# Weight-part stores on SyncE's queue, and a later, denser schedule for the bursts that prepare a slice

## The chip, the cores and the metric

The kernel runs on one core of one Trainium2 chip. The metric is the device time of the program in microseconds (us), smaller is better. Five things matter here: TensorE (PE) multiplies, VectorE (DVE) and ScalarE (ACT) move and cast, GpSimd (POOL) subtracts, and SyncE (SP) only waits and issues DMAs. Each engine takes its instructions strictly in order; they meet at semaphores.

## The reference

```
masked_w = weight * mask[None, :, :]                 # weight (8, 512, 512), mask (512, 512)
w_bot    = einsum('bg,got->bot', y, masked_w)        # y (128, 8): one mixed weight matrix for each of 128 samples
out      = x + (einsum('bnt,bot->bno', x, w_bot) + bias)   # x (128, 128, 512)
```

For each sample b, eight weight matrices are mixed by y[b], and x[b] (128 rows of 512) is multiplied by the mixture; x itself is added (the kernel adds the identity to the weights instead), and a bias. Everything is float32.

## The kernel before

**Tiling.** The 512 outputs are cut into 4 slices of 128, the 128 samples into 4 blocks of 32. A *unit* is a slice of a block; there are 16 units. A unit is 8 *groups* of 4 samples, so there are 128 *steps* n = 0..127, and step n of unit u = n // 8 runs group n. A group is 16 fp32 products, which the profile shows as 32 matmul records (L526), that multiply x (tile `xs`) by the mixed weights in `wbot`. Below, T(n) is the moment at which TensorE begins step n.

**Bursts.** `wbot` of the next unit is made while the current unit runs. That is 8 *bursts* a unit, 4 chunks each (L509, 8 small bf16 matmuls a chunk, 32 a burst), from weight parts in a `ring` of 6 slots against `ydiag`. Burst b belongs to unit b // 8. Within a step TensorE runs the bursts of that step first and then the group. `BEFORE` and `bursts_before(n)` say which bursts stand at step n: one at each step (burst n + 8), except in unit 0, where bursts 8 to 15 stand at steps 3 to 7. The 512-column results lie in 6 PSUM buffers (`S1B`), and are copied to `wbot` by ACT (chunks 0, 1, 3; L348) and DVE (chunk 2; L425). `wbot` is written in place: a chunk (c, k) of the next unit may be written only when sample 4c + k of the current unit has been multiplied (`chunk_ready`). The first group of a unit waits for the last burst's chunks (`evicted`). A third copy, DVE's `duplicate` (L420), fills 32 of the 98 rows of a ring slot from 32 others, and TensorE waits for it.

**Weight parts.** fp32 weights are split into three bf16 parts once, in 32 *tiles* of raw weights, and kept in DRAM (`w_parts`); a unit of a later block reads them again. Four tiles are a *half*, that is the weights of 4 bursts. Units 1, 2, 3, 4 need tiles 0 to 7, 8 to 15, 16 to 23, 24 to 31. A tile goes through: load (`load_raw`, SP), multiply by the mask (`multiply_mask`, DVE, L409), first cast (`cast_w1`, ACT, L330), subtraction (`subtract_w1`, L186), second cast (`cast_w2`, ACT, L334) and second subtraction (`make_w3`, L190), store (`store_parts`, ACT, L342). The subtractions are DVE's for tiles 0 to 7 (`EARLY`) and POOL's afterwards. `TILES_AT` says at which step a tile is cast: tile t at step t - 9 (8 and 9 at step 0), so tile 31 at step 22. Tiles 0 to 7 are done in a prologue, next to the first slice's weights, which are made from `xs` by another path (L488, L490).

**Order of the queues.** SP runs a list written out by hand: first-slice weights, raw tiles, x groups 0 and 1, the first ring loads, and then a loop over n. In its iteration n it loads raw tiles of step n + 2, x groups, and ring slots whose previous burst stands at or before step n. `load_burst` waits until the four tiles of its half are stored (`stored`, L181) and until the slot's previous burst is through TensorE. A raw load (L229) waits until tile t - 8 is done with. ACT runs, per step: second cast of the last step's tile, evictions of chunks 0 and 1, first cast, store of output n - 1 (L353), store of parts, evictions of 2 and 3. DVE runs, per step: `duplicate` of bursts up to `AHEAD` = 2 steps on, mask of the tile, evictions of chunk 2, bias (L436). TensorE's group n waits for x and for the bias of n - 2.

Of the kernel before, what the change touches and what calls it, by code (L numbers as in the profile page):

```python
# [4 lines left out]
P = 128  # L5
# [4 lines left out]
W = 32  # L10
# [10 lines left out]
CO = 16  # L21
CS = SL // CO
OJ = 2
# [21 lines left out]
TILES_AT = {0: (8, 9), **{n: (n + 9,) for n in range(1, 23)}}  # L45
# [4 lines left out]
AHEAD = 2  # L50
BEFORE = {0: (), 1: (), 2: (), 3: (8,), 4: (9,), 5: (10, 11), 6: (12, 13), 7: (14, 15)}
X_AHEAD = 4
# [3 lines left out]
def bursts_before(n):  # L56

    return BEFORE.get(n, (n + GROUPS,) if n + GROUPS < BURSTS else ())
# [13 lines left out]
for _n in range(STEPS):  # L72
    LAST_BURST.append(max((LAST_BURST[-1], *bursts_before(_n))))

# [18 lines left out]
def cond_resid_kernel(nc: bass.Bass, x, w, mask, y, bias, pick, eye, w0, mask0, sel, ident, out, scratch):  # L93
# [6 lines left out]
    with ctx:  # L100
# [16 lines left out]
        sel_sb = sb("sel_sb", [P, CO], fp32)  # L117
        y0_sb = sb("y0_sb", [P, W], fp32)
        ident_sb = sb("ident_sb", [P, P], bf16)
# [14 lines left out]
        s_ident = sem("s_ident")  # L134
# [82 lines left out]
        def _(eng):  # L217
# [19 lines left out]

            def load_burst(b):
# [86 lines left out]
        def _(eng):  # L325
# [10 lines left out]
            def store_parts(t):  # L336
                h, i = divmod(t, PER_HALF)
                eng.wait_ge(s_p2, t + 1)
                p3_made(eng, t)
                at = scratch[h, i * TG, 0, 0, :]  # L340
                to = bass.AP(tensor=at.tensor, offset=at.offset, ap=[[TW, P], [OJ * HCOLS, TG * 3], [1, TW]])
                eng.dma_start(to, parts[:, t % PARTN, :, :, :].rearrange("p g j c -> p (g j) c"))\  # L342
                   .then_inc(s_store[t % PARTN], 16)

# [5 lines left out]
            def store_out(n):  # L350
# [4 lines left out]
            eng.dma_start(y0_sb[:, :], bass.AP(tensor=y.tensor, offset=y.offset,  # L355
                                               ap=[[0, CO], [YC, NG], [1, W]])).then_inc(s_first, 16)
            eng.dma_start(sel_sb[:, :], sel).then_inc(s_first, 16)
            eng.dma_start(ident_sb[:, :].bitcast(fp32), ident).then_inc(s_ident, 16)
# [9 lines left out]
            for c in range(CS):  # L368
                evict(c, 0)
                cast_w1(c)  # L370
                evict(c, 1)
                evict(c, 2)
                cast_w2(c)
                evict(c, 3)
                store_parts(c)
            before = ()
            for n in range(STEPS):
# [12 lines left out]
                for t in before:  # L390
                    store_parts(t)
# [7 lines left out]
            for t in range(TILES - PARTN, TILES):  # L399
                stored(eng, t)  # L400

        @block.vector
        def _(eng):
# [37 lines left out]
            eng.wait_ge(s_first, 16 * 2)  # L441
            eng.tensor_tensor(yblk.rearrange("p (b o) -> p b o", o=CO), y0_sb[:, :].unsqueeze(2).to_broadcast([P, W, CO]),  # L442
# [165 lines left out]
```

## Time and profile before

| | us |
|---|---|
| median of 3 runs | 691.91 |
| lowest, highest | 691.61, 697.16 |
| the profiled execution's own time | 693.39 |
| its span | 691.6 |
| TensorE busy / share | 630.8 / 91% |
| VectorE busy | 371.2 |
| ScalarE busy | 268.8 |
| GpSimd busy | 78.3 |
| mean DMA rate | 231 GB/s |

The span goes from the first to the last instruction; 1.8 us of the execution's time lie around it. Busy times of different engines overlap. "x4096 | 499.1, 281 | 16.6 <-DMA xs<-in_x 13.3" means 4096 instructions, 499.1 us busy in all, 281 ns each (they are pipelined, so the sum is less than count times length), and 16.6 us in which the engine stood idle in front of them, most of it until that DMA.

### The profile page before, as it was taken

The page shows a single profiled execution, that of the slowest core. Times are in us where ns is not written, and L with a number is a line of the kernel's source. Part 1 is how long each engine was busy: PE and PEld are TensorE (multiplying, and loading weights), DVE is VectorE, ACT ScalarE, POOL GpSimd, SP SyncE. Part 2 cuts the span into 40 slices and gives each one's busy share as a digit, 9 for nine tenths or more (in the row PEclk, how much of TensorE's full clock was granted, in tenths as well). Part 3 has the DMA queues.
Part 4 walks back from the last instruction along what each step waited for, and adds up shares of the span by engine and source line. Part 5 has one row for each costly group of instructions (what it writes and reads, how often), then busy time and mean ns, then how long its engine had stood idle before and what let it go on. Part 6 is the DMA issues. An engine that isn't in the chain of part 4 may idle for free.

```text
span 691.6 us, 18831 instructions
## 1 busy us (share of the span) xinstructions
PE 630.8 (91%) x8008; PEld 606.5 (88%) x8008; DVE 371.2 (54%) x433; ACT 268.8 (39%) x449; POOL 78.3 (11%) x63
## 2 busy tenths in 40 slices
PE   5973559989879997999999999999999999999998
PEld 2453559889879987999999999999999999999997
DVE  4734546656765534665565555655565546555421
ACT  3631146445444432343434433343434343434300
POOL 2204422545540000000000000000000000000000
PEclk9996779988989999999999999999999999999999
DMA  9988976777876985655557985555559966553122
GB/s 233 354 252 247 359 253 237 260 233 252 268 239 223 334 294 234 241 208 194 172 184 261 331 290 240 235 189 176 175 191 335 311 243 244 209 191 136 63 77 77
DMA packets 67167, 159.80 MB, mean 231 GB/s; under 512 B 6714, under 2 KB 32412, under 8 KB 55068
## 3 DMA queue, kind: packets, MB, share of 16 engines
q1 hardware_dynamic: 22752, 112.08, 47.3%
q10 hardware_dynamic: 44332, 46.52, 20.0%
q8 instruction: 64, 1.05, 0.6%
q14 instruction: 19, 0.16, 0.1%
HBM read 112.44 MB, written 46.14 MB: 229 GB/s over the span
## 4 chain that ended last, share of the span: by engine, by line
PE 67%; DMA 19%; DVE 4%; SPq 3%; issue 3%; ACTq 2%; ACT 2%; POOL 0%; DVEq 0%
PE ps L526 53%; PE ps L509 13%; DMA ring<-w_parts 8%; DMA raw<-in_w 6%; DMA w_parts<-parts 4%; DMA xs<-in_mask 1%; ACTq L342 1%; DVE raw L409 1%; SPq L255 1%; SPq L256 1%; ACTq L353 1%; ACT wbot L348 1%; DVE wbot L425 1%; DVE raw L186 1%; ACT parts L330 0%
## 5 line engine op out<-in xcount | busy, mean ns | idle before, releaser
L526 PE MATMUL ps<-wbot,xs 128*128 128x128 f32 x4096 | 499.1, 281 | 16.6 <-DMA xs<-in_x 13.3
L526 PEld LDWEIGHTS ps<-wbot,xs 128*128 128x128 f32 x4096 | 478.9, 196 | 18.3 <-DMA xs<-in_x 13.5
L348 ACT ACTIVATE wbot<-ps 128x512 f32<-128x512 f32 x384 | 232.6, 611 | 313.3 <-PE ps L526 269.2
L420 DVE COPY ring<-ring 32x4096 bf16<-32x4096 bf16 x120 | 156.3, 1304 | 62.4 <-DMA ring<-w_parts 59.6
L509 PE MATMUL ps<-ydiag,ring 98*128 98x64 bf16 x3840 | 137.2, 194 | 32.4 <-ACT wbot L348 21.8
L425 DVE COPY wbot<-ps 128x512 f32<-128x512 f32 x128 | 88.2, 690 | 142.7 <-PE ps L526 141.8
L509 PEld LDWEIGHTS ps<-ydiag,ring 98*128 98x128 bf16 x3840 | 131.0, 99 | 37.6 <-ACT wbot L348 24.5
L436 DVE TENSOR_TENSOR staged<-ps,bias_sb 128x512 f32<-128x512 f32 x128 | 88.1, 689 | 41.0 <-PE ps L526 30.0
L409 DVE TENSOR_TENSOR raw<-raw,mask_sb 128x512 f32<-128x512 f32 x32 | 27.3, 856 | 56.5 <-DMA raw<-in_w 56.2
L186 POOL TENSOR_TENSOR raw<-raw,parts 128x512 f32<-128x512 f32 x24 | 29.2, 1218 | 115.7 <-ACT parts L330 115.7
L330 ACT ACTIVATE parts<-raw 128x512 bf16<-128x512 f32 x32 | 20.0, 627 | 55.4 <-DVE raw L409 55.2
L190 POOL TENSOR_TENSOR parts<-raw 128x512 bf16<-128x512 f32 x24 | 40.6, 1692 | 1.9
L488 PE MATMUL ps<-staged,xs 128*128 128x512 f32 x64 | 31.0, 623 | 8.3 <-DMA ident_sb<-in_ident 7.4
L488 PEld LDWEIGHTS ps<-staged,xs 128*128 128x128 f32 x64 | 12.6, 201 | 23.4 <-issue 13.9
L334 ACT ACTIVATE parts<-raw 128x512 bf16<-128x512 bf16 x32 | 20.1, 628 | 15.7 <-POOL raw L186 11.4
L186 DVE TENSOR_TENSOR raw<-raw,parts 128x512 f32<-128x512 f32 x8 | 5.5, 686 | 5.3 <-ACT parts L330 5.3
L414 DVE TENSOR_TENSOR xs<-xs 128x512 f32<-128x512 f32 x8 | 5.6, 698 | 3.6 <-DMA xs<-in_mask 3.6
L190 DVE TENSOR_TENSOR parts<-raw 128x512 bf16<-128x512 f32 x8 | 5.5, 691 | 0.3
L348 ACT ACT_TABLE_LOAD x1 | 1.3, 1283 | 6.7 <-issue 6.7
L442 DVE TENSOR_TENSOR staged<-y_sb,sel_sb 128x512 f32<-128x512 f32 x1 | 0.7, 693 | 5.9 <-DMA sel_sb<-in_sel 5.9
L490 PE MATMUL ps<-ident_sb 128*128 128x512 bf16 x8 | 3.3, 411 | 0.0
L490 PEld LDWEIGHTS ps<-ident_sb 128*128 128x128 bf16 x8 | 0.8, 104 | 2.2 <-issue 2.2
(11 smaller groups left out, 8.8 us busy)
## 6 DMA issues: line engine op xcount, KB each, us to landing
ring<-w_parts SPq DMA_DIRECT2D x240, 256.0 KB
xs<-in_x SPq DMA_DIRECT2D x32, 1024.0 KB, 17.7
out<-staged ACTq DMA_DIRECT2D x128, 256.0 KB, 6.8
w_parts<-parts ACTq DMA_DIRECT2D x32, 384.0 KB, 9.3
raw<-in_w SPq DMA_DIRECT2D x32, 256.0 KB, 10.3
xs<-in_w SPq DMA_DIRECT2D x8, 256.0 KB, 8.2
xs<-in_mask SPq DMA_DIRECT2D x8, 256.0 KB, 9.6
ring<-in_eye SPq DMA_DIRECT2D x120, 16.0 KB
```

The source lines that it names most:

```text
L186: eng.tensor_tensor(at, at, parts[:, t % PARTN, :, 1, :], ALU.subtract).then_inc(done, 1)
L190: eng.tensor_tensor(parts[:, t % PARTN, :, 0, :], raw[:, t % RAWN, :, :], high_half(t), ALU.subtract).then_inc(done, 1)
L330: eng.activation(parts[:, t % PARTN, :, 1, :], raw[:, t % RAWN, :, :], ACT.Copy).then_inc(s_p1, 1)
L334: eng.activation(parts[:, t % PARTN, :, 2, :], high_half(t), ACT.Copy).then_inc(s_p2, 1)
L348: eng.activation(chunk_place(b, k), chunk_sums(b, k), ACT.Copy).then_inc(s_ev_a, 1)
L409: eng.tensor_tensor(at, at, mask_sb[:, h % 2, :].unsqueeze(1).to_broadcast([P, TG, TW]), ALU.mult).then_inc(s_mul, 1)
L420: eng.tensor_copy(ring[QUAD:2 * QUAD, i, :], ring[0:QUAD, i, :]).then_inc(s_dup, 1)
L425: eng.tensor_copy(chunk_place(b, k), chunk_sums(b, k)).then_inc(s_ev_v, 1)
L436: eng.tensor_tensor(staged[:, n % OUTB, :].rearrange("p (b o) -> p b o", b=GB), ps2[n % S2B][:, :].rearrange("p (b o) -> p b o", b=GB), bi ...
L488: ins = eng.matmul(to, xs[:, RAW0 + c, k, :], yblk, start=True, stop=(k > 0))
L509: ins = eng.matmul(ps1[at % S1B][:, g * W * OJ:(g + 1) * W * OJ], ring[:, i, k * CW + g * P:k * CW + (g + 1) * P], ydiag[:, first:first + ...
L526: ins = eng.matmul(ps2[n % S2B][:, b * SL:(b + 1) * SL], xs[:, load % GROUPS * GB + b, k, :], at, start=(k == 0), stop=(k == KT - 1))
```

## The change

- `store_parts` moves from ACT to SP. In the prologue the eight stores stand between the loads: 0 and 1 before x 0, 2 and 3 before x 1, 4 before the first ring load, 5, 6 and 7 between x 2 and x 4. All eight first x groups are now issued in the prologue; the first raw tile after tile 7 (tile 8) comes after all of them and after six ring loads.
- In SP's loop, iteration n first loads raw tiles of step n + 3 (`RAW_AHEAD`), then x, then ring slots, and last stores the tile of step n - 1. A ring load is issued only once the iteration before has issued the stores of its half (`tiles_of`, `kept`).
- `TILES_AT`: tile t is cast at step t - 4, so tiles 8 to 31 stand at steps 4 to 27.
- `LATE`: in units 0 to 3, the bursts of the next unit stand at the unit's steps 2, 3, 4, 5, 6, 6, 7, 7 (none at its steps 0 and 1). From unit 4 on it is one a step, as before.
- `AHEAD` is 1. In the prologue, second casts and second subtractions come one tile later.
- Three small first loads (part of y, `sel`, the identity) become one (`first`). ACT no longer waits for the last stores at the end.

```
-TILES_AT = {0: (8, 9), **{n: (n + 9,) for n in range(1, 23)}}
+TILES_AT = {t - 4: (t,) for t in range(EARLY, TILES)}
-AHEAD = 2
-BEFORE = {0: (), 1: (), 2: (), 3: (8,), 4: (9,), 5: (10, 11), 6: (12, 13), 7: (14, 15)}
-X_AHEAD = 4
+AHEAD = 1
+RAW_AHEAD = 3
+LATE = {0: (0, 0, 1, 1, 1, 1, 2, 2), ... 3: (0, 0, 1, 1, 1, 1, 2, 2)}
 def bursts_before(n):
-    return BEFORE.get(n, (n + GROUPS,) if n + GROUPS < BURSTS else ())
+    u, gg = divmod(n, GROUPS)
+    if u in LATE:
+        first = (u + 1) * CS + sum(LATE[u][:gg])
+        return tuple(range(first, first + LATE[u][gg]))
+    return (n + GROUPS,) if n + GROUPS < BURSTS else ()
+def tiles_of(b):
+    u, c = divmod(b, CS)
+    return (half_of(u % SLICES, c) + 1) * PER_HALF if u <= SLICES else 0
 @block.sync
+            def store_parts(t):                      # was ACT's
+                h, i = divmod(t, PER_HALF)
+                eng.wait_ge(s_p2, t + 1)
+                p3_made(eng, t)
+                ...
+                eng.dma_start(to, parts[:, t % PARTN, :, :, :]...).then_inc(s_store[t % PARTN], 16)
...
+            load_raw(7)
+            store_parts(0)
+            store_parts(1)
             load_x(0)
-            load_raw(7)
+            store_parts(2)
+            store_parts(3)
             load_x(1)
-            for b in range(CS, CS + 4):
-                load_burst(b)
-            load_raw(8)
-            load_raw(9)
+            store_parts(4)
+            load_burst(CS)
             load_x(2)
-            load_raw(10)
+            store_parts(5)
+            load_burst(CS + 1)
             load_x(3)
+            store_parts(6)
+            store_parts(7)
+            load_burst(CS + 2)
+            load_x(4)
+            load_burst(CS + 3)
+            load_x(5)
             load_burst(CS + 4)
+            load_x(6)
             load_burst(CS + 5)
+            load_x(7)
             loaded = CS + RING
+            kept = EARLY
             for n in range(STEPS):
-                for t in TILES_AT.get(n + 2, ()):
+                for t in TILES_AT.get(n + RAW_AHEAD, ()):
                     load_raw(t)
-                if n + X_AHEAD < GROUPS:
-                    load_x(n + X_AHEAD)
                 ...
-                while loaded < BURSTS and loaded - RING <= LAST_BURST[n + 1]:
+                while loaded < BURSTS and loaded - RING <= LAST_BURST[n + 1] and tiles_of(loaded) <= kept:
                     load_burst(loaded)
                     loaded += 1
+                for t in TILES_AT.get(n - 1, ()):
+                    store_parts(t)
+                    kept = t + 1
 @block.scalar
...
-                cast_w2(c)
+                if c:
+                    cast_w2(c - 1)
                 ...
-                store_parts(c)
...
-                for t in before:
-                    store_parts(t)
 @block.vector
...
-                subtract_w1(eng, c, s_rest_v)
-                make_w3(eng, c, s_p3_v)
                 if c + 1 < CS:
                     multiply_mask(c + 1)
+                if c:
+                    make_w3(eng, c - 1, s_p3_v)
+                subtract_w1(eng, c, s_rest_v)
```

## Rows read from the trace of the kernel before

**Rows 1.** The page: TensorE's granted clock in tenths, in 40 slices.
```profile
PEclk9996779988989999999999999999999999999999
```
**Rows 2.** The page: the costliest group, line, engine, count, busy, mean ns, idle before.
```profile
L526 PE MATMUL ps<-wbot,xs 128*128 128x128 f32 x4096 | 499.1, 281 | 16.6 <-DMA xs<-in_x 13.3
```
**Rows 3.** TensorE's timeline in an undisturbed stretch: start us, length us, instruction.
```profile
286.85 1.10 PE L509 MATMUL ps<-ydiag,ring 98*128 98x64 bf16 x32
...
291.44 1.10 PE L509 MATMUL ps<-ydiag,ring 98*128 98x64 bf16 x32
292.37 0.80 PE L526 MATMUL ps<-wbot,xs 128*128 128x128 f32 x5
```
**Rows 4.** TensorE's timeline in unit 0 and at the start of step 8.
```profile
62.56 5.38 PE L526 MATMUL ps<-wbot,xs 128*128 128x128 f32 x32 [13.29 <-DMA xs<-in_x]
...
81.23 1.09 PE L509 MATMUL ps<-ydiag,ring 98*128 98x64 bf16 x16 [8.23 <-ACT wbot L348]
82.13 5.80 PE L526 MATMUL ps<-wbot,xs 128*128 128x128 f32 x32
...
116.06 1.10 PE L509 MATMUL ps<-ydiag,ring 98*128 98x64 bf16 x32
```
**Rows 5.** TensorE's timeline at steps 14, 23 and 32.
```profile
156.69 6.06 PE L526 MATMUL ps<-wbot,xs 128*128 128x128 f32 x32
...
201.09 0.39 PE L509 MATMUL ps<-ydiag,ring 98*128 98x64 bf16 x8 [2.92 <-DVE wbot L425]
...
247.02 1.10 PE L509 MATMUL ps<-ydiag,ring 98*128 98x64 bf16 x32
```
**Rows 6.** VectorE's timeline: a mask that waited for its raw tile.
```profile
151.96 0.69 DVE L409 TENSOR_TENSOR raw<-raw,mask_sb 128x512 f32<-128x512 f32 x1 [7.06 <-DMA raw<-in_w]
```
**Rows 7.** SyncE's waits: line, releaser, us in total, times, longest.
```profile
SPq L181 <- DMA w_parts<-parts: 109.0, 9, 15.8
```
**Rows 8.** Windows: stretch, length, busy of five engines, granted clock, DMA share, GB/s.
```profile
0.00:80.00 80.00, 49.88 (x248) 31.13 (x248) 37.40 (x52) 27.89 (x48) 19.33 (x22) 0.89 0.94 280
34.00:80.00 46.00, 23.27 (x188) 19.39 (x186) 17.11 (x21) 10.87 (x19) 10.78 (x7) 0.81 0.90 270
...
247.00:692.00 445.00, 433.84 (x5890) 431.52 (x5888) 232.79 (x273) 162.20 (x265) 0.00 (x0) 1.00 0.59 210
```
**Rows 9.** The page's DMA queues: SyncE's, packets, MB, share of 16 engines' span.
```profile
q1 hardware_dynamic: 22752, 112.08, 47.3%
```
**Rows 10.** The steps of a tile on ScalarE around the end of step 7.
```profile
115.03 0.62 ACT L330 ACTIVATE parts<-raw 128x512 bf16<-128x512 f32 x1
```
**Rows 11.** The same tile's subtractions on GpSimd, and one slowed beside VectorE.
```profile
115.72 1.16 POOL L186 TENSOR_TENSOR raw<-raw,parts 128x512 f32<-128x512 f32 x1 [4.41 <-ACT parts L330]
116.97 1.04 POOL L190 TENSOR_TENSOR parts<-raw 128x512 bf16<-128x512 f32 x1
...
121.79 1.90 POOL L190 TENSOR_TENSOR parts<-raw 128x512 bf16<-128x512 f32 x1
```
**Rows 12.** Landing times of one store of parts, issued at 120.30 us (tile view).
```profile
DMA to landing us min/median/max: 3.1/3.1/3.1
```
**Rows 13.** Landing time of the store issued at 124.73 us.
```profile
DMA to landing us min/median/max: 15.5/15.5/15.5
```
**Rows 14.** The ring load of burst 16 on SyncE and the duplicate that waited for it.
```profile
101.67 0.67 SPq L255 DMA_DIRECT2D ring<-w_parts  x1
...
106.35 1.22 DVE L420 COPY ring<-ring 32x4096 bf16<-32x4096 bf16 x1 [0.57 <-DMA ring<-w_parts]
```
**Rows 15.** The second loading of x: landing of the load issued at 243.39 us, and TensorE behind it.
```profile
DMA to landing us min/median/max: 29.3/29.3/29.3
...
264.69 1.09 PE L509 MATMUL ps<-ydiag,ring 98*128 98x64 bf16 x32 [1.84 <-DVE wbot L425]
```
**Rows 16.** The page: TensorE's first products, busy, mean ns, idle before.
```profile
L488 PE MATMUL ps<-staged,xs 128*128 128x512 f32 x64 | 31.0, 623 | 8.3 <-DMA ident_sb<-in_ident 7.4
```
**Rows 17.** ScalarE's queue: a DMA issue that took long.
```profile
82.58 6.53 ACTq L353 DMA_DIRECT2D out<-staged  x1
```

More of the change, by code:

```diff
@@ L90, with cond_resid_kernel @@
         A_DONE.append(A_DONE[-1] + (not on_vector(_b, _k)))
-def cond_resid_kernel(nc: bass.Bass, x, w, mask, y, bias, pick, eye, w0, mask0, sel, ident, out, scratch):
+def cond_resid_kernel(nc: bass.Bass, x, w, mask, y, bias, pick, eye, w0, mask0, first, out, scratch):
     fp32 = mybir.dt.float32
@@ L116, in cond_resid_kernel @@
         ydiag = sb("ydiag", [KALL, NB, OJ], bf16)
-        sel_sb = sb("sel_sb", [P, CO], fp32)
-        y0_sb = sb("y0_sb", [P, W], fp32)
-        ident_sb = sb("ident_sb", [P, P], bf16)
+        first_sb = sb("first_sb", [P, W + CO + P // 2], fp32)
+        y0_sb = first_sb[:, 0:W]
+        sel_sb = first_sb[:, W:W + CO]
+        ident_sb = first_sb[:, W + CO:].bitcast(bf16)
         bias_sb = sb("bias_sb", [P, NO], fp32)
@@ L236, in load_first @@
                    .then_inc(s_w0[c], 16)
+            def store_parts(t):
+                h, i = divmod(t, PER_HALF)
+                eng.wait_ge(s_p2, t + 1)
+                p3_made(eng, t)
+                at = scratch[h, i * TG, 0, 0, :]
+                to = bass.AP(tensor=at.tensor, offset=at.offset, ap=[[TW, P], [OJ * HCOLS, TG * 3], [1, TW]])
+                eng.dma_start(to, parts[:, t % PARTN, :, :, :].rearrange("p g j c -> p (g j) c"))\
+                   .then_inc(s_store[t % PARTN], 16)
             def load_burst(b):
@@ L353, in store_out @@
                 eng.dma_start(out[u, :, gg, :], staged[:, n % OUTB, :]).then_inc(s_out[n % OUTB], 16)
[L355 to L358, printed above, removed]
+            eng.dma_start(first_sb[:, :], first).then_inc(s_first, 16)
             for q in range(3):
@@ L398, in _ @@
                 eng.wait_ge(s_out[i], 16 * (STEPS // OUTB))
-            for t in range(TILES - PARTN, TILES):
-                stored(eng, t)
         @block.vector
@@ L439, in add_bias @@
                                   ALU.add).then_inc(s_o, 1)
[L441 to L443 removed]
+            eng.wait_ge(s_first, 16)
+            eng.tensor_tensor(yblk.rearrange("p (b o) -> p b o", o=CO), y0_sb.unsqueeze(2).to_broadcast([P, W, CO]),
+                              sel_sb.unsqueeze(1).to_broadcast([P, W, CO]), ALU.mult).then_inc(s_yblk, 1)
             multiply_first(0)
@@ L482, in first_burst @@
                     eng.wait_ge(s_yblk, 1)
-                    eng.wait_ge(s_ident, 16)
+                    eng.wait_ge(s_first, 16)
                 eng.wait_ge(s_mul0, c + 1)
@@ L567 @@
     }
-    a["sel"] = np.repeat(np.eye(CO, dtype=np.float32), NG, axis=0)
-    a["ident"] = np.where(np.eye(P), 0x3F80, 0).astype(np.uint16).view(np.float32)
+    ident = np.where(np.eye(P), 0x3F80, 0).astype(np.uint16).view(np.float32)
+    a["first"] = np.concatenate([np.tile(y[:, :W], (CO, 1)), np.repeat(np.eye(CO, dtype=np.float32), NG, axis=0), ident],
+                                axis=1)
     pick = np.zeros((KALL, 3 + OJ), np.float32)
@@ L598 @@
     cond_resid_kernel(nc, aps["x"], aps["w"], aps["mask"], aps["y"], aps["bias"], aps["pick"], aps["eye"],
-                      aps["w0"], aps["mask0"], aps["sel"], aps["ident"], out, scratch)
+                      aps["w0"], aps["mask0"], aps["first"], out, scratch)
     r = run_bass_kernel_spmd(nc, [arrays], core_ids=[0])
```

15 lines of the change are left out of this document (4 added, 11 removed).

## The prediction

> **What bounds the kernel now.** I read the page's slices first: after the first third TensorE's clock stands at 9 or more everywhere, before it it falls to 6 again and again [rows 1]. The costliest group is the fp32 product, and nearly all its waiting is one wait for x [rows 2]. So I asked TensorE's timeline what a step costs when nothing disturbs it: bursts begin at 286.85 and 291.44 and the group behind the latter at 292.37, so a step is 4.59 us, of which the burst is 0.94 and the group 3.65 [rows 3]. From step 32 on the kernel is that and little else: 433.8 of 445 us busy [rows 8]. All that a schedule can win lies ahead of it, in two stretches.
>
> Opening, up to T(8) = 116.1. TensorE stood 13.3 us for x 2, 8.2 us for an eviction behind a blocked ScalarE queue, and more of that kind [rows 4]. After such a wait a group takes 5.80 instead of 3.82 us as the timeline counts it, about 2.0 more: these are the two levels, 1.2 and 2.4 GHz, of the granted clock, which is 0.89 of full on average up to 80 us and 0.81 from 34 to 80, while the DMA engines are 0.94 busy up to 80 us, at 280 GB/s [rows 4, 8].
>
> Steps 8 to 31, from 116.1 to T(32) = 247.0: 130.9 us [rows 4, 5], where 24 steps of 4.59 are 110.2. The 20.7 us more are visible as VectorE waiting for a raw tile that SyncE loaded late (7.06 us at 151.96), with evictions and bias behind it in its queue [rows 6]; TensorE then waits for the eviction, 2.92 us at step 23 [rows 5]. SyncE was late because it stood 109 us in nine waits until a half was stored [rows 7].
>
> **The change, part by part.**
>
> *Opening.* x 2 no longer stands behind four ring loads and three raw tiles, so its 13.3 us go. What is late next is tile 8. It is cast at step 4, and its load now stands behind all eight x groups and six ring loads. What must have moved by then: first weights and their masks 4.2 MB, raw tiles 0 to 8 with masks 2.6, x 8.4, ring 3.1, stores of eight tiles 3.1, outputs of five steps 1.3: 22.7 MB (1 KB = 1024 B; sizes are the tiles' own). In the old kernel 80 us moved 280 GB/s, 22.4 MB [rows 8], so it lands at L = 80; I take 79, since there is slightly less of slow small stuff on the queues. TensorE has nothing to wait for before step 6 (step 0 at about 40 as before, then two groups alone and four steps of 4.59, and some loss between the slices: about 67) and then stands: VectorE's step 4 waits for tile 8, and behind it in its queue are the eviction of burst 10, the bias of step 4 (for group 6) and the duplicates of bursts 12 and 13. From L on VectorE needs 0.69 for the mask, 0.69 eviction, 0.69 bias, 1.22 each for two duplicates, 0.69 mask of tile 9; ScalarE casts it (0.62), waits for GpSimd's 1.16 and casts again (0.62) before it evicts burst 12, which burst 13 needs. That is 9.1 us from L to the start of group 6. Then 5.8 for the cold group, and 5.5 for step 7 with its two bursts: T(8) = L + 20.5 = 99.5. **Term: -16.5.** Bounds: at 344 GB/s (112.08 MB in 47.3% of 691.6 us, SyncE's queue [rows 9]) from about 35 us, L is 69 and the term -26.5; with 270 GB/s, the rate between 34 and 80 us [rows 8], and 4 us of idle DMA while SyncE waits for stores 3 and 7, L is 87 and the term -8.5.
>
> *The round trip of a half, six times.* This is the heart of it. The first half of units 2, 3 and 4 ends with a tile cast at the last step of a unit and is needed by a burst at the next unit's step 2; the second half ends at step 3 and is needed at step 6. In the old schedule there were six steps between, now three. Take tile 11, step 7, burst 16 at step 10. ScalarE's first cast stands behind the eviction of the second burst's chunk 1, which must wait for sample 29; in the old trace the cast of that step stands at 115.03, 1.03 us before T(8) [rows 4, 10]. GpSimd's subtractions are 1.16 and 1.04 or 1.90 us; the second of step 7's tile ended at 118.0, 1.95 after T(8) [rows 11]. I say T(8) + 2.4 for the store. A store with nothing behind it landed in 3.1 us [rows 12]; with loads issued behind and around it, in 15.5 [rows 13]. Here SyncE stands still behind the store, so 3.3. Then 0.4 for waking and the small identity load, 4.65 from the issue of the ring load until its duplicate could start [rows 14], 1.22 for the duplicate: T(8) + 12.1. Steps 8 and 9 now have no bursts and last 3.65 each, so TensorE is there at T(8) + 7.3. It waits 4.8 (the last evictions of the old unit, which no burst covers any more at steps 8, 16 and 24, lie inside that), and then runs a group at the low clock, 2.0.
>
> Second half, tile 15, step 11, bursts 20 and 21 at step 14: VectorE's step 11 starts 0.8 after T(11), duplicate 1.22, mask 0.69, cast 0.62, subtractions 1.16 and 1.90: store at T(11) + 6.3; 3.3 + 0.4 + 4.65 + 1.22 make 16.0, against 13.8 for three steps: 2.2. But VectorE was held in step 13, with the mask of tile 17 behind the duplicates, and TensorE needs for burst 21 what ScalarE evicts of burst 20 only after the second cast of tile 17: after the mask about 4.7 us go by until the group starts (in the old trace mask at 151.96, group at 156.69 [rows 5, 6]). So group 14 starts 6.5 us after burst 20 instead of 1.9: 4.6 more, and again 2.0 for the clock. A unit pays 4.8 + 2.0 + 2.2 + 4.6 + 2.0 = 15.6, three units **46.8**.
>
> Bounds of this term: with the store landing at 3.1 and a ring load at 3.5 (my estimate: little more than such a store), it is still 30; with 6.4 and 6 us for the two it is 75. Nothing excludes the lower end, and no gain is in it.
>
> *The second x loads in unit 3.* They are issued at steps 25 to 32. In the old kernel no tile was under way then; now half four is stored and read back at steps 24 to 30, on the same queue, behind up to three x groups of 1 MB. Loads of x landed there after up to 29.3 us [rows 15]. I put 3 us on the first half and 8 on the second: **11**, between 3 and 20.
>
> *What goes.* The 20.7 us of steps 8 to 31 go in full: raw tiles are now loaded before SyncE stands for the stores, three steps ahead, and a load that finds the queue empty has three steps. So steps 8 to 31 take 110.2 + 46.8 + 11 = 168.0 instead of 130.9: **+37.1**.
>
> *After step 32.* The old kernel loses 11.2 us there [rows 8], most of it in waits of 1 to 2 us behind the x loads, where VectorE stood for a ring slot it needed only two steps on [rows 15]. `AHEAD` of 1 makes it stand one step later. **-6**, between 0 and -9.
>
> *Edits taken together at nothing.* One first load for three: TensorE waited 7.4 us for the identity [rows 16], and its first product needs the masked first weights, ready at about the same time; within 0.3. The store waits at the end of ScalarE's queue were long over. Moving 32 issues off ScalarE frees its queue: but the outputs stay there, and one of them held the queue 6.53 us [rows 17]; what held TensorE in the opening is counted above. The Trainium skill, page DMA: Bandwidth & Descriptors, section Issuing engines are not separate DMA queues, says that issuing from several engines saves only the time of issue. By that rule alone the move would change no landing time and would be worth the few long issues; the rows say otherwise, 3.1 against 15.5 us for a store of the same size [rows 12, 13], so I let a store's landing depend on what is queued with it.
>
> **Sum:** -16.5 + 37.1 - 6 = +14.6. Against the profiled execution, 693.4, that is 708.0; it was 1.5 above the median, so on the median's scale 706.5. I say **706**.
>
> **Rivals.**
>
> *A, the round trip is hidden (faster).* Place: from the first cast of a half's last tile to the duplicate of its first burst. It decides whether these take less than 9.2 us (first half) or 13.8 from the step's start. For it: the 4.65 us of the ring load is a single reading, and an empty queue could be quicker. Against: cast, subtractions and one store landing alone are 6 us, which leaves 3 for a ring load and its duplicate [rows 10 to 12]. Then the 46.8 fall away: 706 - 47 = 659. Chance 0.10.
>
> *B, DMA is quicker than I allow.* L is 69, x is absorbed in unit 3 (3 instead of 11), ring loads land in 3.5: -10 - 8 - 7: 681. For it: x-heavy stretches of the page move over 340 GB/s. Chance 0.18.
>
> *C, stores behind loads.* SyncE's list puts a store behind whatever was issued before it: the six critical stores land in 6.4 or more, ring loads in 6, x in unit 3 costs 20: by the upper bounds above 706 + 28 + 9; not all six will meet them, say 728. For it: the 15.5 of [rows 13] and 29.3 of [rows 15]. The Trainium skill, same page, section Queues, rings and completion order, says that each ring is consumed in order and an engine takes turns between queue rows: a store on ScalarE's queue would get its turn beside the loads, on SyncE's it stands behind them. That would be this case. Chance 0.15.
>
> *D, the schedule changes nothing measurable* (what the opening wins the halves take): 692. Chance 0.09.
>
> **How the numbers follow.** My forecast, 693 to 720, has 0.48. The likeliest is the sum, 706. Two in ten are left out by a range from 674 (below B; it leaves out A) to 729 (the upper part of C goes). A change within 1% of 692, that is 685 to 699, is about what this kernel's measurement cannot tell from none: from D 0.09 and the lower fringe of the forecast 0.10, with 0.01 of B: 0.20. Faster by over 1%: A 0.10, B 0.15: 0.25. Slower: the rest, 0.55.
>
> **What would show it.** T(8) near 100, with VectorE's L409 waiting for a raw tile until about 79 and no wait of TensorE for x 2. In steps 8 to 31, SyncE's waits at L181 short and regular, and VectorE's duplicate waiting for a ring load just before steps 10, 14, 18, 22, 26 and 30, each followed by one group of about 5.8 us. T(32) near 268. Granted clock below 0.96 over all. If TensorE runs through steps 10 and 14 without a wait, A holds and the forecast is wrong; if T(8) lies below 92, the opening was sized wrong; if the waits at steps 26 and 30 are no longer than those at 10 and 14, the x term was.

## The result, and the profile after

The changed kernel takes 714.5 us (median of 4 runs, 711.4 to 720.2) against 693.7 for the kernel before (4 runs): ratio 1.030, 95% interval 1.022 to 1.039. It is slower, as forecast, and by more: 706 was said. The 691.9 of the table above is the median of the first three runs of the kernel before; its fourth run took 695.5. The profiled execution took 713.9, its span is 712.1, 20.5 more than before.

The page of the kernel after: TensorE's granted clock, and the groups of the fp32 product, the ring duplicate, the burst and the mask.

```profile
PEclk9987769978978969999999999999999999999999
...
L546 PE MATMUL ps<-wbot,xs 128*128 128x128 f32 x4096 | 504.1, 284 | 4.6 <-DMA xs<-in_x 3.7
...
L438 DVE COPY ring<-ring 32x4096 bf16<-32x4096 bf16 x120 | 154.1, 1285 | 78.7 <-DMA ring<-w_parts 75.7
L529 PE MATMUL ps<-ydiag,ring 98*128 98x64 bf16 x3840 | 138.2, 196 | 58.0 <-DVE ring L438 25.8
...
L427 DVE TENSOR_TENSOR raw<-raw,mask_sb 128x512 f32<-128x512 f32 x32 | 24.2, 758 | 18.9 <-DMA raw<-in_w 18.4
```

The last three groups in the kernel before, from its page:

```profile
L420 DVE COPY ring<-ring 32x4096 bf16<-32x4096 bf16 x120 | 156.3, 1304 | 62.4 <-DMA ring<-w_parts 59.6
L509 PE MATMUL ps<-ydiag,ring 98*128 98x64 bf16 x3840 | 137.2, 194 | 32.4 <-ACT wbot L348 21.8
L409 DVE TENSOR_TENSOR raw<-raw,mask_sb 128x512 f32<-128x512 f32 x32 | 27.3, 856 | 56.5 <-DMA raw<-in_w 56.2
```

TensorE's idle time in front of the fp32 product shrank from 16.6 to 4.6 us, the part that was a wait for x from 13.3 to 3.7 [rows 2]. In its place it stands 58.0 us in front of bursts, where it was 32.4. VectorE's waits for ring loads grew from 59.6 to 75.7 us, while those for raw tiles fell from 56.2 to 18.4, nearly all of it one single wait.

Windows of the kernel after, cut at the steps of the new kernel (step 8 begins at about 108.2, step 32 at 275.5): stretch, length, busy of five engines, granted clock, DMA share, GB/s.

```profile
0.00:80.00 80.00, 64.48 (x392) 44.88 (x392) 34.73 (x51) 27.94 (x49) 8.25 (x15) 0.91 0.95 277
...
80.00:108.20 28.20, 14.30 (x192) 13.94 (x193) 15.69 (x17) 12.11 (x22) 8.63 (x7) 0.70 0.63 213
108.20:275.50 167.30, 128.38 (x1539) 125.94 (x1538) 82.45 (x94) 63.80 (x113) 51.31 (x42) 0.85 0.72 237
275.50:712.10 436.60, 432.99 (x5890) 431.38 (x5887) 233.66 (x273) 162.21 (x265) 0.00 (x0) 1.00 0.59 211
```

So the 20.5 us are made of three numbers. Up to step 8 the kernel gained 7.9 (108.2 against 116.1, [rows 4]). Steps 8 to 31 take 167.3 instead of 130.9, 36.4 more. From step 32 on it takes 436.6 instead of 444.6, 8.0 less ([rows 5, 8]).

The opening: TensorE's timeline from step 4 on, and VectorE's mask of tile 8.

```profile
74.81 3.84 PE L546 MATMUL ps<-wbot,xs 128*128 128x128 f32 x32
91.29 1.87 PE L529 MATMUL ps<-ydiag,ring 98*128 98x64 bf16 x32 [12.64 <-DVE ring L438]
94.48 1.08 PE L529 MATMUL ps<-ydiag,ring 98*128 98x64 bf16 x16 [1.32 <-DVE wbot L443]
96.85 1.09 PE L529 MATMUL ps<-ydiag,ring 98*128 98x64 bf16 x16 [1.28 <-ACT wbot L372]
97.75 5.10 PE L546 MATMUL ps<-wbot,xs 128*128 128x128 f32 x32
```

```profile
87.30 0.69 DVE L427 TENSOR_TENSOR raw<-raw,mask_sb 128x512 f32<-128x512 f32 x1 [16.57 <-DMA raw<-in_w]
```

The first half's round trip. SyncE's store of tile 11 and ring load of burst 16, as the chain of waits between 108 and 121 us of the kernel after has them (start, length, what):

```profile
107.88 1.18 POOL raw L197
...
109.12 1.49 POOL parts L201
...
110.67 2.97 DMA w_parts<-parts
...
114.10 0.68 SPq L275
...
114.83 4.72 DMA ring<-w_parts
...
119.64 1.09 PE ps L529 x32
```

A ring slot is filled by two loads. The duplicate needs the first, issued at 114.10; TensorE also needs the second, issued at 114.83, and that one landed last. The duplicate of burst 16 on VectorE:

```profile
118.07 1.22 DVE L438 COPY ring<-ring 32x4096 bf16<-32x4096 bf16 x1 [4.96 <-DMA ring<-w_parts]
```

TensorE at steps 10, 11, 14, 26 and 30 of the kernel after, with what it waited for:

```profile
119.64 1.09 PE L529 MATMUL ps<-ydiag,ring 98*128 98x64 bf16 x32 [3.69 <-DMA ring<-w_parts]
120.57 5.45 PE L546 MATMUL ps<-wbot,xs 128*128 128x128 f32 x32
125.85 1.10 PE L529 MATMUL ps<-ydiag,ring 98*128 98x64 bf16 x32
...
142.52 1.09 PE L529 MATMUL ps<-ydiag,ring 98*128 98x64 bf16 x32 [2.74 <-DVE ring L438]
146.46 1.09 PE L529 MATMUL ps<-ydiag,ring 98*128 98x64 bf16 x16 [2.84 <-DVE wbot L443]
148.82 1.11 PE L529 MATMUL ps<-ydiag,ring 98*128 98x64 bf16 x16 [1.27 <-ACT wbot L372]
149.74 6.35 PE L546 MATMUL ps<-wbot,xs 128*128 128x128 f32 x32
...
228.80 1.86 PE L529 MATMUL ps<-ydiag,ring 98*128 98x64 bf16 x32 [4.76 <-DMA ring<-w_parts]
...
259.97 1.87 PE L529 MATMUL ps<-ydiag,ring 98*128 98x64 bf16 x32 [10.44 <-DVE ring L438]
```

The wait before step 10 is followed by a group of 5.45 us, the pair of bursts at step 14 takes from 142.52 to 149.74, and the group behind it 6.35. The same pattern stands at steps 18 and 22. In unit 3 the waits are longer, but the pair of bursts takes only 5.1 us (259.97 to 265.03).

### The profile page after: what moved, and what is told of

Its sections match the earlier page's. It is cut to its first block, busy times and chain, and to the rows that moved or that the text cites. A ratio compares the mean times of both kernels' runs of the same rounds, so it can differ in the third digit from the quotient of the medians.

```text
span 712.1 us, 18826 instructions
## 1 busy us (share of the span) xinstructions
PE 640.1 (90%) x8008; PEld 616.2 (87%) x8008; DVE 366.5 (51%) x433; ACT 266.1 (37%) x449; POOL 68.2 (10%) x63
## 2 busy tenths in 40 slices
DMA packets 66880, 159.81 MB, mean 224 GB/s; under 512 B 6426, under 2 KB 32124, under 8 KB 54780
## 4 chain that ended last, share of the span: by engine, by line
PE 71%; DMA 19%; SPq 3%; POOL 2%; issue 2%; DVE 2%; ACT 1%; ACTq 0%; DVEq 0%
PE ps L546 54%; PE ps L529 14%; DMA ring<-w_parts 9%; DMA w_parts<-parts 7%; DMA raw<-in_w 3%; PE ps L508 3%; POOL raw L197 1%; SPq L275 1%; DVE ring L438 1%; POOL parts L201 1%; ACT parts L363 1%; SPq L276 1%; SPq L268 1%; DMA xs<-in_mask 1%; DVE raw L427 0%
## 5 line engine op out<-in xcount | busy, mean ns | idle before, releaser
L546 PEld LDWEIGHTS ps<-wbot,xs 128*128 128x128 f32 x4096 | 484.9, 198 | 6.2 <-DMA xs<-in_x 4.0
L372 ACT ACTIVATE wbot<-ps 128x512 f32<-128x512 f32 x384 | 229.9, 611 | 310.5 <-PE ps L546 249.6
L438 DVE COPY ring<-ring 32x4096 bf16<-32x4096 bf16 x120 | 154.1, 1285 | 78.7 <-DMA ring<-w_parts 75.7
L529 PEld LDWEIGHTS ps<-ydiag,ring 98*128 98x128 bf16 x3840 | 133.3, 100 | 62.1 <-issue 56.2
L363 ACT ACTIVATE parts<-raw 128x512 bf16<-128x512 f32 x32 | 20.1, 627 | 79.0 <-DVE raw L427 78.8
L427 DVE TENSOR_TENSOR raw<-raw,mask_sb 128x512 f32<-128x512 f32 x32 | 24.2, 758 | 18.9 <-DMA raw<-in_w 18.4
L201 POOL TENSOR_TENSOR parts<-raw 128x512 bf16<-128x512 f32 x24 | 32.3, 1345 | 1.9
L508 PEld LDWEIGHTS ps<-staged,xs 128*128 128x128 f32 x64 | 12.8, 205 | 22.0 <-issue 13.8
L367 ACT ACTIVATE parts<-raw 128x512 bf16<-128x512 bf16 x32 | 20.1, 629 | 19.5 <-POOL raw L197 19.3
L510 PE MATMUL ps<-first_sb 128*128 128x512 bf16 x8 | 3.3, 411 | 0.0
L347 POOL TENSOR_SCALAR staged<-staged,pick_sb 98x128 bf16<-98x128 bf16 x3 | 3.0, 995 | 0.3
```

Source lines behind the costliest of these rows:

```text
L201: eng.tensor_tensor(parts[:, t % PARTN, :, 0, :], raw[:, t % RAWN, :, :], high_half(t), ALU.subtract).then_inc(done, 1)
L363: eng.activation(parts[:, t % PARTN, :, 1, :], raw[:, t % RAWN, :, :], ACT.Copy).then_inc(s_p1, 1)
L367: eng.activation(parts[:, t % PARTN, :, 2, :], high_half(t), ACT.Copy).then_inc(s_p2, 1)
L372: eng.activation(chunk_place(b, k), chunk_sums(b, k), ACT.Copy).then_inc(s_ev_a, 1)
L427: eng.tensor_tensor(at, at, mask_sb[:, h % 2, :].unsqueeze(1).to_broadcast([P, TG, TW]), ALU.mult).then_inc(s_mul, 1)
L438: eng.tensor_copy(ring[QUAD:2 * QUAD, i, :], ring[0:QUAD, i, :]).then_inc(s_dup, 1)
```

## Experiments

Ratios are against the kernel before, run beside it on the same chip; its median was 692 to 694 each time. Where a text below splits a total into "up to step 8", "steps 8 to 31" and "from step 32 on", the times are read from TensorE's timeline of the profiled run.

**1. Bursts later.**

```
-LATE = {... 1: (0, 0, 1, 1, 1, 1, 2, 2), 2: (same), 3: (same)}
+LATE = {... 1: (0, 0, 0, 1, 1, 2, 2, 2), 2: (same), 3: (same)}
```

> The changed kernel with the bursts of units 1 to 3 one step later at two places: at the unit's steps 3, 4, 5, 5, 6, 6, 7, 7 instead of 2, 3, 4, 5, 6, 6, 7, 7. Theory 1 (the round trip of a half, from the last tile's cast to the duplicate, is a fixed time of about 11.4 us after step 8, 16, 24 begins, and TensorE waits for what is left of it): the first half gets one step of 3.65 us more, so the waits of 3.7, 3.6 and 4.8 us at steps 10, 18, 26 shrink to about 0, 0 and 1 at steps 11, 19, 27, and with them the low clock behind them (some 2 us each); the second half stays. Saving 15 to 18 us: about 697 on the scale on which the changed kernel has 714.5. Theory 2 (rival: the waits are a shortage of DMA time, so that a later burst is late as well): 712 to 716, with waits of the same length one step later. Theory 3 (two bursts in a step cost more where more steps have them): 716 to 722.

Measured: 716.6, ratio 1.033 (1.029 to 1.037). None of the three, though the total looks like the second. The first half did gain: TensorE's wait shrank from 3.69 to 2.02 us and group 11 came 4 us earlier after step 8. Then the second half took it back. TensorE and SyncE of this kernel around steps 11 to 14:

```profile
121.87 1.09 PE L529 MATMUL ps<-ydiag,ring 98*128 98x64 bf16 x32 [2.02 <-DVE ring L438]
...
148.71 3.57 PE L529 MATMUL ps<-ydiag,ring 98*128 98x64 bf16 x64 [5.95 <-DVE wbot L443]
```

```profile
124.87 4.62 SPq L240 DMA_DIRECT2D raw<-in_w  x1
...
132.43 1.57 SPq L255 DMA_DIRECT2D w_parts<-parts  x1
```

In the changed kernel the store of tile 15 went out 6.5 us after step 11 began (132.34 against 125.85); here, at 132.43, 10.6 us after (121.87). SyncE was held by its own issues: 4.6 us for one raw tile, with four bursts' ring loads, two stores and another raw tile issued just before. The store itself then landed in 6.3 us, where 4.4 had been enough. What TensorE waited for at the end stands behind that on VectorE: the eviction at 147.88 comes after both duplicates of step 14 in its queue. So the trip is not a fixed time. My reading is that the less TensorE waits, the fuller the DMA queues are for the next trip; no run here shows that by itself.

**2. Tile 8 early.** Raw tiles 8, 9 and 10 are loaded behind x group 4.

```
             load_x(4)
+            for t in (8, 9, 10):
+                load_raw(t)
```

> The changed kernel with raw tiles 8, 9 and 10 loaded after x group 4 in the prologue instead of behind x 7 and six ring loads. Theory 1 (the 12.6 us in which TensorE stood before step 6 came from VectorE's queue, where the mask of tile 8 waited for its load until 87.3 us): the mask waits little, TensorE waits for x 6 and x 7 instead, which land some 3 us later than at 80 and 86 us; step 8 starts at 96 to 102 instead of 108.2, total 702 to 709. Theory 2 (the opening is bound by the DMA volume as a whole, so that the order does not matter): step 8 starts at 106 to 109, total 712 to 716.

Measured: 707.5, ratio 1.021 (1.018 to 1.024). The first theory holds. TensorE's wait before step 6 is gone; it waits 4.71 us for VectorE in the middle of step 6, and then runs on:

```profile
80.34 1.10 PE L532 MATMUL ps<-ydiag,ring 98*128 98x64 bf16 x32
86.14 1.08 PE L532 MATMUL ps<-ydiag,ring 98*128 98x64 bf16 x16 [4.71 <-DVE wbot L446]
...
97.86 4.49 PE L549 MATMUL ps<-wbot,xs 128*128 128x128 f32 x38
```

Group 7 starts at 97.9 instead of 104.6, and the total is 7 us less. Steps 8 to 31 are as they were: 167.4 us against 167.3.

**3. Tiles two steps earlier.** Experiment 2 and `TILES_AT = {t - 6: (t,) ...}`.

> As the kernel with tiles 8, 9 and 10 loaded early, and every tile from 8 on is cast two steps earlier (tile t at step t - 6, steps 2 to 25). Theory 1 (round trips): the six waits before steps 10, 14, 18, 22, 26, 30 vanish, as the trip of 11 to 16 us now has 15.6 to 23 us; what ScalarE and VectorE held back at the two-burst steps goes too. Steps 8 to 31 fall from 167 to 112 to 120 us; step 8 starts at 96 to 104. Total 650 to 664, faster than the kernel before. Theory 2 (stores on SyncE's queue are slow in themselves, and SyncE waiting for them holds back the raw loads): waits appear at other places, total 690 to 710.

Measured: 698.6, ratio 1.009 (1.006 to 1.012): 9 us less than experiment 2, not 45. This is the cleanest test of the slack, since nothing differs from experiment 2 but the step of the casts, and with it that of the raw loads and the stores. Steps 8 to 31 fell by 20.1 us, from 167.4 to 147.3, where 47 to 55 had been forecast; step 8 came 3.3 us later (104.8 against 101.5), and from step 32 on the kernel took 445.0 instead of 436.8 us, so that the 8 us gained there were gone. The waits before steps 10 and 18 are gone, as forecast; TensorE still waits 2.8 us before step 14 and again in its pair of bursts, and raw tiles come late again. VectorE and SyncE of this kernel:

```profile
123.63 0.69 DVE L430 TENSOR_TENSOR raw<-raw,mask_sb 128x512 f32<-128x512 f32 x1 [4.50 <-DMA raw<-in_w]
```

```profile
115.48 4.26 SPq L240 DMA_DIRECT2D raw<-in_w  x1
```

The total lies in the second theory's range, and its late raw tiles are there; the first theory's mechanism holds for the waits before steps 10 and 18. Before step 30 TensorE still waits 8.7 us.

**4. Paced ring loads.** Experiment 3 and, up to step 31, `loaded <= LAST_BURST[n + 4]` as one more condition of a ring load.

> As the kernel with tiles cast two steps earlier (698.6), and up to step 31 a ring load is issued only for bursts that stand at most three steps on, instead of four loads in a row as soon as a half is stored. Theory 1 (four ring loads in a row, 2 MB, fill the DMA queues, hold SyncE's next issues for up to 4.6 us and let raw tiles and stores land 7 to 10 us later, which is why the earlier tiles gave less than reckoned): steps 8 to 23 fall from 96 to 80 to 88 us, total 684 to 692. Theory 2 (the sum of the traffic is the limit, not its order): 696 to 701.

Measured: 700.2, ratio 1.013 (1.005 to 1.021), no better than experiment 3. Steps 8 to 23 took 96 us in both, where 80 to 88 was forecast. This reordering of the ring loads does not help. That the sum of the traffic is the limit does not follow: experiments 7 and 8 move the same bytes and gain.

**5. Look-ahead alone.** The kernel before with `AHEAD = 1`.

> The kernel before with one edit: the look-ahead of the duplicates is 1 instead of 2. Theory 1 (the 8 us that the changed kernel gains after step 32 come from VectorE standing one step later for a ring slot that is delayed by x loads): the stretch from step 32 to the end falls from 444.6 to about 437, total 683 to 686 on the scale on which the kernel before has 692; little changes ahead of it. Theory 2 (the gain after step 32 comes from the x loads falling in TensorE's waits, where the DMA can catch up): no change, 690 to 694.

Measured: 695.0, ratio 1.002 (0.999 to 1.005): no difference. The windows from step 32 on, of this kernel:

```profile
247.80:694.20 446.40, 433.61 (x5889) 431.35 (x5887) 233.25 (x272) 162.09 (x265) 0.00 (x0) 1.00 0.60 210
```

12.8 us without TensorE, where the kernel before has 11.2 [rows 8]. So in this schedule the look-ahead gives nothing. Experiments 3 and 9 agree: both have a look-ahead of 1 and take 445.0 and 444.5 us from step 32 on, like the kernel before with 444.6, and not 436.6. Where the 8.0 us of the changed kernel come from is not shown. The second theory would have it that x, loaded from step 25 on, lands while TensorE waits 10.4 us before step 30. Against it, experiment 9 takes 51.8 us for steps 24 to 31 (36.7 in the kernel before) and gains nothing behind them.

**6. Stores back on ScalarE.** `store_parts` in ScalarE's list again, behind the output store; all else as changed.

> The changed kernel with one part undone: the stores of parts are issued by ScalarE again, behind the output store of a step. Everything else (late tiles, late bursts, the order of the loads, a ring load only after its half) stays. Theory 1 (on SyncE the critical store went out 2.4 and 6.5 us after the step, on ScalarE it stands behind the next tile's first cast and the output): each of the six trips is 1 to 2 us longer, total 717 to 725. Theory 2 (the issuing queue matters for the time of issue alone): 711 to 717. Theory 3 (rival: SyncE's waits for the casts and its long issues cost more than they give): 700 to 710.

Measured: 716.4, ratio 1.037 (1.031 to 1.043), against 1.030 (1.022 to 1.039): the intervals overlap. It lies in the second theory's range. The part of the change that stands first in its description is not what made the kernel slower; in this schedule it moves the time by a few us at most.

**7 and 8. Another layout of the weight parts.** In both kernels a ring load reads 8 blocks of 4 rows. If the parts lie part by part, its 32 rows are one evenly spaced dimension; a tile then needs two stores.

```
-scratch = nc.dram_tensor("w_parts", (HALVES, NG, 3, OJ, HCOLS), ...)
+scratch = nc.dram_tensor("w_parts", (HALVES, 3, NG, OJ, HCOLS), ...)
-                w1_w2 = bass.AP(..., ap=[[3 * OJ * row, NG], [row, 2 * OJ], [1, BW]])
+                w1_w2 = bass.AP(..., ap=[[row, QUAD], [1, BW]])
...
-                eng.dma_start(to, parts[:, t % PARTN, :, :, :]...)
+                for g in range(TG): ... eng.dma_start(to, parts[:, t % PARTN, g, :, :])
```

> The changed kernel with the weight parts laid out in DRAM by part, then group, so that the 32 rows of a ring load are one evenly spaced dimension, not 8 blocks of 4; the price is two stores for a tile instead of one. Theory 1 (a ring load runs on half of the 16 DMA engines, by the Trainium skill's rule on how many engines a DMA uses, and these are full up to about step 32 while the others are not; in the trace the mean DMA share is 0.6 while x loads and ring loads pile up): ring loads take half the time, SyncE's long issues and the late landings shrink; the first raw tile lands at 70 to 77 instead of 87 us, each of the six trips is 1 to 2 us shorter, the wait before step 30 falls from 12 to about 5: 680 to 695. Theory 2 (the engines as a whole are the limit, or the trips are latency alone): 709 to 716, the two stores costing what the layout gives.

> The kernel before with the same layout of the weight parts and two stores a tile. Theory 1 (half of the DMA engines are full up to step 34): 660 to 680. Theory 2 (latency alone): 688 to 696; it may even be slower, since ScalarE has 32 issues more.

Measured: the changed kernel so altered 704.8, ratio 1.018 (1.012 to 1.025); the kernel before 681.2, ratio 0.984 (0.977 to 0.992). Both gain, by 10 and 13 us: the slowest run of each altered kernel lies below the fastest of the kernel that it was made from. The second theory is out in both cases, and the first promised more than came. In the changed kernel the mask of tile 8 began at 84.1 instead of 87.3 us, where 70 to 77 had been forecast, and steps 8 to 31 took 160.8 us instead of 167.3. The window from 110 to 247 us, first of the kernel before, then of the kernel before with the layout:

```profile
110.00:247.00 137.00, 126.08 (x1638) 123.59 (x1637) 83.50 (x90) 65.41 (x111) 48.65 (x34) 0.94 0.78 259
```

```profile
110.00:247.00 137.00, 127.00 (x1677) 124.44 (x1677) 87.10 (x90) 62.98 (x110) 45.94 (x31) 0.98 0.95 265
```

The DMA engines' mean share went from 0.78 to 0.95. The Trainium skill, page DMA: Bandwidth & Descriptors, section Why a DMA increments its semaphore by 16 and not by 1, says that a DMA runs on the largest number of engines up to 16 that divides the slowest dimension of both its sides: 8 for the old ring load, 16 for the new. The profile's counts of packets bear it out, first of the kernel before, then of the kernel before with the layout:

```profile
DMA packets 67167, 159.80 MB, mean 231 GB/s; under 512 B 6714, under 2 KB 32412, under 8 KB 55068
```

```profile
DMA packets 69623, 159.81 MB, mean 235 GB/s; under 512 B 9170, under 2 KB 34868, under 8 KB 57524
```

The bytes are the same, and all 2456 packets more are under 512 B. An estimate that gives each DMA one such packet for each engine that it runs on hits this exactly: 8 more for each of the 240 ring loads are 1920, the 32 stores more have 16 each, 512, and three more small loads of y have 8 each, 24. The changed kernel has 2456 more as well (6426 and 8882). So the old ring load ran on 8 engines and the new one on 16. That these 8 were full while the others were not is not shown, as no row has an engine by itself. Nor is it separated from the stores, which the same edit cuts from one of 384 KB into two of 192 KB.

**9 to 11. The change without its late schedule.** Stores on SyncE, `kept`, `AHEAD` and most of the prologue stay; raw tiles 8 to 11 are now loaded between the x groups, as in experiment 2. The edit below is that of experiments 9 and 10 (experiment 10 with the new layout too).

```
-TILES_AT = {t - 4: (t,) for t in range(EARLY, TILES)}
+TILES_AT = {t - 7: (t,) for t in range(EARLY, TILES)}
-LATE = {0: (0, 0, 1, 1, 1, 1, 2, 2), 1: (same), 2: (same), 3: (same)}
+LATE = {0: (0, 0, 1, 1, 1, 1, 2, 2)}
```

> The changed kernel (stores on SyncE, its prologue, a ring load only after its half, look-ahead 1) without its late schedule: tile t is cast at step t - 7 (steps 1 to 24), bursts stand one a step from unit 1 on, and raw tiles 8 to 11 are loaded between x groups 1 to 4. Theory 1 (the late schedule is what made the kernel slower: six trips with 11 to 16 us for 7 to 14 us of steps): a half now has at least four steps, 18 us; steps 8 to 31 take 120 to 135 us instead of 167, step 8 starts at 100 to 108, total 672 to 690, no slower than the kernel before. Theory 2 (it is the queue: SyncE carrying all traffic in one order): 700 to 715.

> The same with the weight parts laid out so that a ring load is one evenly spaced dimension of 32 rows (two stores a tile). Theory (two causes that add: late halves and ring loads on half of the DMA engines): 10 to 20 us below the kernel without the layout, 655 to 675, faster than the kernel before and than that one with the new layout (681). Rival (the DMA engines as a whole are full by then): 672 to 682.

> The new layout, raw tiles 8 to 11 loaded between x groups 2 to 5, tiles cast at step t - 5 (8 to 19), t - 6 (20 to 23) and t - 7 (24 to 31), bursts late in units 0 to 2 as in the changed kernel and one a step from unit 3 on. Theory (a half has four steps, the late bursts of units 1 and 2 then cost nothing, and the opening waits for x alone): 660 to 678, within 6 of the kernel with early halves. Rival (two bursts in a step with a duplicate and a cast ahead of them cost 4 to 5 us each time, whatever the slack): 678 to 690.

Measured: 694.6 in the old layout, ratio 1.0025 (1.0003 to 1.005), the same as the kernel before for all purposes; in the new layout 670.4, ratio 0.967 (0.964 to 0.971), 24 us below, more than the 10 to 20 forecast, with the total within its range; the middle schedule in the new layout 673.2, ratio 0.971 (0.967 to 0.975). So the late schedule and the late raw tiles 8 to 11 together cost the changed kernel 20 us in the old layout (714.5 to 694.6), and 34 in the new one (704.8 to 670.4). In the old layout 7 of them are what experiment 2 had already shown for the raw tiles, and the schedule's share is about 13.

The first theory of experiment 9 holds in its direction only. Steps 8 to 31 fell from 167.3 to 144.8 us, where 120 to 135 was forecast, and from step 32 on 7.9 us were lost again. TensorE still waited for ring loads, before steps 16 and 24 above all:

```profile
158.08 1.87 PE L534 MATMUL ps<-ydiag,ring 98*128 98x64 bf16 x32 [5.66 <-DMA ring<-w_parts]
...
205.80 1.87 PE L534 MATMUL ps<-ydiag,ring 98*128 98x64 bf16 x32 [6.06 <-DMA ring<-w_parts]
```

The kernel before takes 130.9 us for these steps; experiment 9 is even with it only because its step 8 comes 9.5 us earlier (106.6). In the new layout steps 8 to 31 take 125.1 us. The middle schedule lies within the theory, not the rival, although its pair of bursts at step 14 still costs 7 us. The same window of the fastest kernel:

```profile
110.00:247.00 137.00, 125.97 (x1724) 124.71 (x1724) 91.17 (x96) 65.10 (x113) 45.74 (x33) 0.99 0.99 299
```

The engines are 0.99 busy at 299 GB/s. By that share the DMA has nothing left to give in this stretch, and I take the traffic to be its bound. But the share alone does not prove it: it was 0.95 at 265 GB/s in experiment 8, so it does not measure bytes.

**12. The fastest kernel with its stores on ScalarE.**

> The fastest kernel so far (early halves and the new layout, 670.4) with the stores of parts issued by ScalarE again. The DMA engines are 0.97 to 0.99 busy in it up to step 32, so the traffic as a whole is the limit. Theory 1 (which queue issues the stores hardly matters, with late halves or without): 667 to 675. Theory 2 (the stores on SyncE, in their order between the loads, are worth something once halves have slack; on ScalarE a full DMA queue holds up its evictions): 677 to 688. Theory 3 (a store on its own queue gets its turn beside the loads, halves are there earlier): 658 to 667.

Measured: 676.4, ratio 0.975 (0.972 to 0.979) against 0.967 (0.964 to 0.971). It lies between the first two theories' ranges, and the stores on SyncE are worth about 6 us here. Step 8 begins at the same time (101.2 us); steps 8 to 31 take 131.9 instead of 125.1 us. Its window:

```profile
110.00:247.00 137.00, 125.27 (x1616) 123.98 (x1616) 85.88 (x92) 61.98 (x108) 43.07 (x32) 0.93 0.96 277
```

ScalarE's issues of stores took up to 2.8 us here for a pair.

## Why the prediction came out as it did

The side and the mechanism were right; the time, 706, lay 8.5 below the measured 714.5, inside the range. One term was mis-sized, the opening. Between the profiled runs the sum gave +14.6 and 20.5 was measured, 5.9 more: the opening gave 8.6 too little, steps 8 to 31 took 0.7 less than forecast, and the stretch after step 32 gave 2.0 more. The other 2.6 us of the 8.5 come from the scale: 1.5 and 0.5 were taken off for the median and in rounding, and the median lies 0.6 above the profiled run. By its steps:

- **The six round trips.** Forecast for steps 8 to 31: 168.0 us; measured 167.3. First half: store at T(8) + 2.4, duplicate done at + 12.1; measured 110.67, that is + 2.5, duplicate done at + 11.1, and TensorE's burst at + 11.4, behind the second ring load, which the forecast left out. Second half: burst at T(11) + 16.0; measured 142.52 - 125.85 = 16.7. The pair of bursts before group 14: 6.5; measured 7.2. The landings were 3.0 and 4.4 us where 3.3 was taken; from the issue of the first ring load to the duplicate it took 4.0 where 4.65 was taken. That the total came within a microsecond is partly luck: a unit without waits takes 36.7 us, and over that the three units paid 16.5, 18.1 and 22.5 us, where 15.6, 15.6 and 26.6 were forecast. (The group at 156.69 us in [rows 5] is that of step 15, not 14; the 4.7 us read from it stand.) The lower bound of the term, 30, is mis-reckoned too: a ring load in 3.5 us and a store in 3.1 take 1.35 off each trip and leave about 39. Experiment 3 shows the cause: two more steps for a half take the waits before steps 10 and 18 away and 20.1 of the 57.1 us. The other 37 stay, in waits behind late raw tiles and full queues. What the argument lacked is that the trip depends on what stands in the queue ahead of it: experiments 1, 3 and 9 gave back far less than the sum of the waits. That the waits were also a breathing space for the DMA fits these runs, but is argued and not shown.
- **The opening: the step that was mis-sized.** The mechanism was as written, the mask of tile 8 holding VectorE and with it TensorE before step 6. But L was put at 79 and the tile landed at 87.3; from there to step 8 it was 20.9 us against the 20.5 reckoned. The term was -7.9, not -16.5; that these 8.6 us come so near to the whole miss of 8.5 is chance, as said above. The sum took the mean rate of the whole core, 280 GB/s, for the 22.7 MB ahead of tile 8. Up to 80 us that rate held (277), but behind it the engines were no longer full, although tile 8 had been queued since 65.4 us:

```profile
80.00:87.30 7.30, 0.00 (x0) 0.00 (x0) 0.00 (x1) 0.00 (x0) 0.00 (x0) 0.73 0.67 238
```

By 87.3 us 23.9 MB had moved (274 GB/s), 1.2 more than the sum counted. A queue whose ring loads run on 8 of 16 engines is not drained by volume alone, and the new layout brought the mask of tile 8 from 87.3 to 84.1 and step 8 from 108.2 to 106.1; the rest of the 8 us is open. Experiment 2 shows that the place of tile 8 cost 7 us. One more step of the forecast failed without being seen in the time: TensorE was to be ready for step 6 at about 67 us and was at 78.7, after four shorter waits of 1.3 to 2.5 us, two of them for x, and slow groups of 6.5 us behind two. The wait for tile 8 covered it.
- **x in unit 3.** Forecast 3 and 8 us over the other units' waits; the waits before steps 26 and 30 were 4.8 and 10.4 against 3.7 and 2.7: 1 and 8. The store of tile 31 landed in 12.2 us, with x groups issued ahead of it. But the pair of bursts at step 30 took 2 us less than in unit 1, and unit 3 as a whole paid only 4.4 to 6.0 us over the other two, not 11.
- **After step 32: the right size for the wrong reason.** Forecast -6, measured -8.0; but I gave it to the look-ahead, and experiments 3, 5 and 9 show that a look-ahead of 1 does not bring it. Getting the size was luck. Steps 24 to 39 took 81 us in the kernel before and 96 in the changed one, so the 8 us are no gain over this stretch; where they come from is open.
- **The store's queue.** I let a store's landing depend on its company and gave the move itself no term. Experiment 6 agrees: nothing clear. The rule of the Trainium skill, page DMA: Bandwidth & Descriptors, section Issuing engines are not separate DMA queues, that it saves issue time alone would have given the same here; experiment 12 shows 6 us in a kernel whose DMA share is 0.99.
- **Rivals.** A (the trip is hidden) fails by the waits at all six places. B fails by L, 87.3 and not 69; its quick ring loads and cheap x in unit 3 came nearer. C fails by the landings, which were 2.7 to 4.5 us at five of the six critical stores; the last, behind x in unit 3, took 12.2, as C has it. D fails by the time.

## What to carry to other kernels

When a producer's store and a consumer's load meet in DRAM, write the round trip down in full, with everything each engine has ahead in its queue, and compare it with the steps the schedule leaves: moving work "late, in order of need" takes away exactly that slack. Do not expect to win back the sum of such waits by giving slack: here two steps more for every half gave back 20 of 57 us where they stood, and 9 in the total. Look first at whether the loads use all the engines: here the shape of one load in DRAM, with the stores cut in two that it needs, was worth 10 to 24 us, and with it and halves that have slack the kernel takes 670 us against 693.

## What the runs showed of the hardware

A store of 384 KB landed in 3.0 us when nothing but a mask and a raw tile was issued right behind it, and in 9 to 13 us just behind four bursts' ring loads or with x loads around it. The issue of one DMA held SyncE's queue for up to 4.6 us, behind four bursts' ring loads, another raw tile and two stores. The profile tells on how many engines a load runs, by an estimate that gives each DMA one packet under 512 B for each of its engines. In the kernel before these are 240 ring loads with 8, 120 loads of identity rows with 2, 252 DMAs of 128 rows with 16 and 40 for the last few small loads, and 482 short rows of data come on top: 6714, the profile's own count. The same sum gives 9170 with the new layout, again the profile's count. Spreading the ring loads raised the DMA engines' mean share from 0.78 to 0.95 at nearly the same rate, 259 and 265 GB/s: the same bytes kept the engines busy longer, which the number of engines does not explain, and which stays open. The fastest kernel moved 299 GB/s at a share of 0.99.
